# A decoder step on one core: the turn of the keys moved ahead of the feed-forward product, the window mask written by TensorE instead of ScalarE

## The reference, cut to what matters

```python
q = l2norm(q) * qs                     # per head of 64; k in the same way
q = q * cos * scale + rotate_half(q) * sin * scale
sim = einsum('bhwie,bhwje->bhwij', bq, bk2) * QK_SCALE   # windows of 32, keys of own and last window
sim = where(mask, -finfo.max, sim)
attn = softmax(sim, -1)
out = einsum('bhwij,bhwje->bhwie', attn, bv2)
x = attn_layer(shift_tokens(x), ...) + x
x = ffn_layer(shift_tokens(x), ...) + x      # ffn: layernorm * g + b, W1, a * gelu(gate), W2
```

## Time and profile before

| what | us |
|---|---|
| three runs, median | 2246.75 (2243.56 to 2249.29) |
| the profiled execution | 2244.96 |
| its span, first to last instruction | 2243.2 |
| busy: PE / DVE / ACT / POOL | 2034.3 / 1359.3 / 1328.8 / 1079.3 |

### The profile page before, as it was taken

The page is one execution under the profiler, slowest core; times in us unless marked ns, Lnnn a source line. Parts: engine busy times, 40 slices in busy tenths (PEclk is TensorE's granted clock), DMA queues, the critical chain, the costliest instruction groups (busy, mean ns, idle before and its releaser), DMA issues.

```text
span 2243.2 us, 73622 instructions
## 1 busy us (share of the span) xinstructions
PE 2034.3 (91%) x32680; PEld 1198.6 (53%) x32680; DVE 1359.3 (61%) x1663; ACT 1328.8 (59%) x1640; POOL 1079.3 (48%) x708
## 2 busy tenths in 40 slices
PE   8999998779999999999999999999999999999987
PEld 4655655345555555555555555555555555555553
DVE  1444444566666666666766666666676666666662
ACT  4444354365666666656666666666666666666664
POOL 0000000377555555655656555655565656555550
PEclk9999999799999999999999999999999999999999
DMA  3000000022223222232322222222222223222220
GB/s 104 2 1 1 2 19 29 19 58 67 59 60 94 68 68 58 59 87 58 77 59 59 77 68 74 62 58 67 78 75 66 62 59 96 68 67 59 59 58 20
DMA packets 81912, 128.04 MB, mean 57 GB/s; under 512 B 17214, under 2 KB 28092, under 8 KB 81468
## 3 DMA queue, kind: packets, MB, share of 16 engines
q1 hardware_dynamic: 81596, 123.33, 21.2%
HBM read 21.55 MB, written 1.05 MB: 10 GB/s over the span
## 4 chain that ended last, share of the span: by engine, by line
PE 66%; ACT 14%; issue 8%; DVE 7%; POOL 3%; SPq 0%; POOLq 0%; DMA 0%; ACTq 0%; DVEq 0%
PE ps L598 14%; PE ps L624 8%; PE ps L602 7%; PE ps L662 5%; PE ps L679 5%; PE ps L655 5%; ACT KT L962 4%; PE ps L414 4%; PE ps L642 3%; PE ps L607 2%; PE ps L611 2%; DVE work L1055 2%; POOL work L1377 2%; DVE work L1052 2%; ACT ps L953 2%
## 5 line engine op out<-in xcount | busy, mean ns | idle before, releaser
L1377 POOL TENSOR_TENSOR work<-work,RS 128x1024 f32<-128x1024 f32 x192 | 361.6, 1904 | 313.3 <-ACT RS L996 313.3
L602 PEld LDWEIGHTS ps<-ident,work 128*128 128x128 f32 x3072 | 343.6, 142 | 149.3 <-issue 71.0
L1052 DVE TENSOR_TENSOR work<-ps,work 128x1024 f32<-128x1024 f32 x192 | 230.8, 1202 | 311.4 <-ACT work L975 300.0
L602 PE MATMUL ps<-ident,work 128*128 128x128 f32 x3072 | 392.7, 276 | 27.0 <-ACT work L949 12.2
L1371 POOL TENSOR_TENSOR work<-work 128x1024 f32<-128x1024 f32 x96 | 226.2, 2356 | 370.0 <-DVE work L1055 370.0
L598 PE MATMUL ps<-WK,XS 128*128 128x512 f32 x384 | 189.5, 616 | 51.0 <-ACT KT L962 51.0
L1055 DVE TENSOR_TENSOR work<-ps,work 128x1024 f32<-128x1024 f32 x192 | 233.1, 1214 | 0.0
L1091 DVE TENSOR_REDUCE SS<-work 128x16 f32<-128x1024 f32 x192 | 232.1, 1209 | 0.0
L1364 POOL TENSOR_TENSOR work<-work 128x1024 f32<-128x1024 f32 x96 | 226.1, 2355 | 5.7 <-DVE work L1055 5.7
L662 PEld LDWEIGHTS ps<-work 64*32 64x32 f32 x12288 | 136.0, 106 | 163.2 <-issue 106.2
L922 ACT ACTIVATE work<-ps 128x1024 f32<-128x1024 f32 x96 | 98.1, 1022 | 208.7 <-PE ps L662 206.9
(11 more groups left out here) (184 smaller groups left out, 3102.2 us busy)
## 6 DMA issues: line engine op xcount, KB each, us to landing
work<-work SPq DMA_DIRECT2D x576, 128.0 KB
work<-work SPq DMA_DIRECT2D x336, 64.0 KB
WQ<-in_wqkv SPq DMA_DIRECT2D x6, 512.0 KB, 3.6
WK<-in_wqkv SPq DMA_DIRECT2D x6, 512.0 KB, 4.2
WV<-in_wqkv SPq DMA_DIRECT2D x6, 512.0 KB, 3.6
WO<-in_wo SPq DMA_DIRECT2D x6, 512.0 KB, 3.8
work<-ZR SPq DMA_DIRECT2D x48, 64.0 KB
W<-in_w SPq DMA_DIRECT2D x6, 341.0 KB, 3.0
```

What stands on the lines that cost most here:

```text
L602: m = nc.tensor.transpose(flat(R)[:, t * 128:t * 128 + 128], src[:, t * 128:t * 128 + 128], ident[:, :])
L1052: V.tensor_tensor(h16(cos_part[:, j, :]), h16(flat(src)), rotary_tabs[:, at:at + 64].unsqueeze(1).broadcast_to([PARTS, 16, 64]), ALU.mult) ...
L1377: U.tensor_tensor(h16(qk_norm[:, j, :]), h16(cos_part[:, j, :]), inv_norms[:, j, :].unsqueeze(2).broadcast_to([PARTS, 16, 64]), ALU.mult). ...
```

## The change

It changes the order of instructions and moves two pieces of work to another engine:

- PE: the turn of the heads goes ahead of the V projection. The turn of the keys goes ahead of the feed-forward piece, right behind the V projection. The turn of the queries and the K projection stay behind the feed-forward piece.
- The mask: ACT's copy L953 goes. PE puts the mask into bank_x with two bf16 matmuls of 128 x 512 (identity times a broadcast mask) behind the K projection and ahead of the scores; for this the mask is copied to bf16 once by DVE, and PE waits on `values_copied`.
- ACT: the copy of the turned heads (L949) goes ahead of the copy of the values (L942). The load of the gelu table at n = 1 goes behind the copy of the turned keys. `ffn_affine` goes; DVE's `norm` multiplies by g at once and adds b in a second instruction.
- Feed-forward at n = 1: PE makes `hid(1)` whole behind the scores, then the gate of chunk 2 between the weighing's halves and its value at the end. DVE's `gated(1)` goes behind the scores' shift.

```diff
 # PE, step
+                if d:
+                    pe.wait_ge(heads_copied, g - 2)
+                    turn(bank_y, heads).then_inc(heads_turned, 1)
                 if b:
                     pe.wait_ge(wv_loaded, 16 * ((g - 1) // 16 + 1))
...
                     m.then_inc(values_ready, 1)
-                if d:
-                    pe.wait_ge(heads_copied, g - 2)
-                    turn(bank_y, heads).then_inc(heads_turned, 1)
+                if b:
+                    pe.wait_ge(k_normed, g)
+                    if d:
+                        pe.wait_ge(heads_turned_copied, g - 2)
+                    turn(bank_y, qk_norm[:, 1, :]).then_inc(k_turned, 1)
                 if f is not None and n == 0:
                     centre(f)
...
                 if b:
-                    pe.wait_ge(k_normed, g)
-                    if d:
-                        pe.wait_ge(heads_turned_copied, g - 2)
-                    turn(bank_y, qk_norm[:, 1, :]).then_inc(k_turned, 1)
                     if a:
                         pe.wait_ge(q_sin, g + 1)
                     pe.wait_ge(q_normed, g)
...
                     pe.wait_ge(k_turned_copied, g)
                     pe.wait_ge(q_turned_copied, g)
-                    pe.wait_ge(mask_seeded, g)
+                    pe.wait_ge(mask_ready, 1)
+                    pe.wait_ge(values_copied, g)
+                    for q in range(2):
+                        mm(bank_x[:, q, :].rearrange('p (c k) -> p c k', k=64), ident_bf16[:, :], window_bf16[:, 0 if nb == 0 else 1, :].unsqueeze(1).broadcast_to([PARTS, 8, 64]), start=True, stop=False, skip_group_check=True)
...
                     pe.wait_ge(hidden_gated, 3 * f + 1)
-                    hid_gate(1, bank_f)
+                    hid(1, bank_f)
...
-                    hid_value(1, bank_f)
+                    pe.wait_ge(gate_gelu, 3 * f + 2)
+                    hid_gate(2, bank_f)
...
                     pe.wait_ge(hidden_gated, 3 * f + 2)
-                    hid(2, bank_f)
+                    hid_value(2, bank_f)
 # ACT, step
-                if f is not None and n == 1:
-                    ffn_affine(f)
...
-                if b:
-                    act.wait_ge(values_ready, g)
-                    if due(g - 1):
-                        act.wait_ge(windows_loaded, 160 * (g - 1))
-                    A(v_rows[:, (n - 1) % 2, :], flat(bank_x), ACT.Copy).then_inc(values_copied, 1)
                 if d:
                     act.wait_ge(heads_turned, g - 2)
...
                 if b:
-                    act.wait_ge(values_copied, g)
-                    seed = window_mask[:, 0 if n == 1 else 1, :]
-                    A(bank_x.rearrange('p q (c k) -> p (q c) k', k=64), seed.unsqueeze(1).broadcast_to([PARTS, 16, 64]), ACT.Copy).then_inc(mask_seeded, 1)
+                    act.wait_ge(values_ready, g)
+                    if due(g - 1):
+                        act.wait_ge(windows_loaded, 160 * (g - 1))
+                    A(v_rows[:, (n - 1) % 2, :], flat(bank_x), ACT.Copy).then_inc(values_copied, 1)
                 if f is not None and n == 0:
                     square(f)
-                if f is not None and n == 1:
-                    nc.scalar.preload_act_table_set(GELU)
                 if b:
                     act.wait_ge(k_turned, g)
...
+                if f is not None and n == 1:
+                    nc.scalar.preload_act_table_set(GELU)
 # DVE
             def norm(f):
                 dve.wait_ge(ffn_inverse, f + 1)
                 if due(f):
-                    dve.wait_ge(ffn_input, f)
-                V.tensor_tensor(normed[:, :], bank_f[:, 1, :], spread[:, :], ALU.mult).then_inc(ffn_normed, 1)
+                    dve.wait_ge(hidden_ready, 3 * f)
+                V.scalar_tensor_tensor(out=normed[:, :], in0=bank_f[:, 1, :], scalar=layer_vecs[:, f // 4 * 9 + 6:f // 4 * 9 + 7], in1=spread[:, :], op0=ALU.mult, op1=ALU.mult).then_inc(ffn_normed, 1)
+                dve.wait_ge(ffn_normed, f + 1)
+                V.tensor_scalar(ffn_in[:, :], normed[:, :], layer_vecs[:, f // 4 * 9 + 7:f // 4 * 9 + 8], None, ALU.add).then_inc(ffn_input, 1)
...
-                if f is not None and n == 1:
-                    gated(f, 1, bank_f)
                 if b:
                     dve.wait_ge(scores_ready, g)
...
+                if f is not None and n == 1:
+                    gated(f, 1, bank_f)
                 if a:
                     sums(1, k_squared, k_sums, g)
```

More of the change, by code:

```diff
@@ L146, in decoder @@
     ident_bf16 = nc.alloc_sbuf_tensor('ident_bf16', [PARTS, 128], BF16)
+    window_bf16 = nc.alloc_sbuf_tensor('wmb', [PARTS, 2, 64], BF16)
     causal_bf16_mask = nc.alloc_sbuf_tensor('mkb', [PARTS, 128], BF16)
@@ L293, in decoder @@
     windows_loaded = nc.alloc_semaphore('windows_loaded')
-    mask_seeded = nc.alloc_semaphore('mask_seeded')
+    mask_ready = nc.alloc_semaphore('mask_ready')
     q_sums = nc.alloc_semaphore('q_sums')
@@ L910, in inverse @@
                 A(spread[:, :], spread[:, :], ACT.Exp, scale=-0.5).then_inc(ffn_inverse, 1)
[L912 to L916, removed]
             def copy_heads(g):
@@ L1322, in _ @@
             dve.wait_ge(constants_loaded, 16 * 9)
+            V.tensor_copy(window_bf16[:, :, :], window_mask[:, :, :]).then_inc(mask_ready, 1)
             cross()
```

## The result

The changed kernel takes 2351.23 us (median; 2335.81 to 2354.75), against 2246.49 for the kernel before timed beside it: a ratio of 1.0455, with a 95% interval of 1.0417 to 1.0494. It is slower, as forecast, and 21 us above the predicted 2330. The profiled execution took 2347.74 us with a span of 2345.3 (before: 2244.96 and 2243.2).

What follows compares the result with a forecast made beforehand. PE's program order bounds the kernel. Steps n = 0 to 3 change by + 0.90, - 0.46, + 2.34, + 1.11, + 3.89 per pass, + 85.6 over 22; early steps + 1, "issue" - 3: 2330 us, range 2298 to 2368.

Steps and rivals of the forecast that it cites:

- The main step: Keys' turn ahead of the feed-forward piece: PE stands still 1.0, 1.4, 2.1, 1.0 us for POOL's keys at n = 0 to 3.
- The mask: Two bf16 matmuls on PE ahead of the scores: 0.52 us added at n = 1, 2 and 3, hidden at n = 0.
- The regrouping at n = 1: Feed-forward behind the K projection at n = 1: gating wait of 0.70 us per pass ends, about 0.1 new gelu wait.
- The 3 us taken off for "issue": PE's waits that no engine explains, some 21 us: 3 us taken off the sum as falling into the waits for POOL.
- The heads' turn ahead of the values: Heads' turn ahead of the V projection on PE, with ACT's copies swapped: free, as the heads' copy is done before the keys.
- DVE's added instruction: DVE's addition per pass, 0.54 us, at the end of n = 0: costs nothing; 13 us without its cover.
- The ends: The parts before and behind the steps: they don't change by 1 us.
- 1 us earlier: Rival: POOL's pair comes 1 us earlier in every step, so it evens out at 2243 us; chance 0.03.
- The clock's rival: Rival: the wait at n = 2 also lowers PE's clock in every pass, 1.65 us each, 36 in all, 2366; chance 0.14.
- The sign set for the clock's rival: If the waits for POOL are there and the full passes' granted clock is below 0.98, the clock's rival is the case.
- The rival that DVE slows POOL: Rival: DVE's addition slows POOL's product at n = 1 by 0.54 us, 12 us over the passes, 2342; chance 0.04.
- The first rival: Rival: ACT, relieved of the mask copy, gives inverse norms earlier; PE never waits for POOL, 39 us faster, 2205; chance 0.08.

Runs made afterwards that it cites:

- the fastest version: Changed kernel with the keys' turn back behind the feed-forward piece, mask ahead of the K projection, gelu's table load behind ACT's copy of queries at n = 1: 2198.15 us.

## Why the prediction held, and where its sizes were off

**The main step held to about a tenth of a microsecond.** The turn waits for POOL in every step, because POOL's pair starts where it did. The forecast put the K projection at t0 + 9.07, 9.37, 10.95 and 9.82; the undisturbed steps have 9.05, 9.50, 10.96 and 9.79. At n = 1 it is 0.13 later because POOL's pair takes 3.88 us there and not 3.77 (see the small terms). The wait of the projection for ACT's copy stayed at n = 0 alone, 0.82 us, behind the square. The waits for POOL add up to 108 us, not 120: a wait counts only from the end of the last product's tail, 0.17 us after the point from which the prediction counted. That changes no start.

"Undisturbed" in the table means a step without an "issue" pause and without a drop of the clock, behind a step that has none either.

| step | before | forecast | after, undisturbed |
|---|---|---|---|
| n = 0 | 16.26 | 17.16 | 17.14 |
| n = 1 | 20.55 | 20.09 | 19.84 |
| n = 2 | 18.16 | 20.50 | 20.36 |
| n = 3 | 17.40 | 18.51 | 18.32 |
| pass | 72.37 | 76.26 | 75.66 |

**The mask was priced too high.** The pair does hold the scores back by 0.53 us (1774.52 to 1775.05), as the row said. But directly behind the projection it starts 1.72 us after the projection's start, while the scores before came 1.89 after it (1776.80 to 1778.69): the product's tail of 0.17 now lies under the mask. That is 0.36 net at n = 2, and so at n = 1 and n = 3, where 0.52 was put in; over the passes 0.16 x 3 x 22 = 10.6 us too much. The scores before, at n = 1 and 2:

```profile
1758.75 0.86 PE L655 MATMUL ps<-KT,work 64*32 64x64 f32 x64
...
1778.69 0.86 PE L655 MATMUL ps<-KT,work 64*32 64x64 f32 x64
```

The estimate of 0.43 by the Trainium skill's issue gap ("TensorE: Matmul & The Clock Gate", Back-to-back issue gap) lies between the two, the 0.53 and the 0.36.

**The regrouping at n = 1 gave a little more.** From the K projection to the end of the step it takes 10.34 us undisturbed (19.84 - 9.50), where 10.72 was forecast. Of the difference 0.16 is the mask again (2.24 us from the projection to the scores, 1750.81 to 1753.05, against 1.88 before, 1756.87 to 1758.75), 0.1 is the new wait on the gelu, which doesn't show at all, and 0.08 is that the wait taken away was 0.78 in the pass used, not 0.70. That leaves 0.04.

**The clock was the largest mis-sized term.** The undisturbed passes explain 3.29 x 22 = 72.4 of the 92.8 us, where 85.6 were forecast; drops of the clock explain 22.1 - 3.4 = 18.7; some 2 I can't assign. The prediction had the price right (1.65 against 1.70 per drop), but treated the drop as a separate case, all or none, and left it out of the sum, since the clock had stayed up behind 1.85 us in an early step. It came in 13 passes of 22. So part of the near hit is luck, two errors against each other: 13 us too much for the steps (10.6 of them the mask), 19 too little for the clock.

**Small terms.** The 3 us taken off for "issue" were wrong: 21.5 us before, 21.1 after. The heads' turn ahead of the values was costed at nothing, and rightly, given the swap on ACT; the run with the turn alone has neither, and there PE waits 92.5 us for the heads' copy. DVE's added instruction does slow POOL, but little. In 6 of the 22 passes the addition (0.49 us) runs on into the first product of POOL's pair at n = 1, by 0.22 to 0.27 us, and that product takes 1.98 to 2.03 us; where they overlap by 0.05 or less, it takes 1.90, as it always did before. In the pass shown:

```profile
1743.12 0.49 DVE L1075 TENSOR_SCALAR YN<-YR,vec 128x512 f32<-128x512 f32 x1
```

That is 0.12 us where the rival put 0.54, and some 0.7 us over all passes where it put 12, so that the mean of POOL's products barely moves (1908 ns, 1905 before). The Trainium skill ("GPSIMD Engine Reference", Key points) has POOL contend with certain of DVE's instructions; the trace agrees, with 2.03 us against 1.90.

The ends were forecast unchanged and grew by 9.3 us: 3.4 in the attention stage ahead, which the change doesn't touch, 2.1 in the first eight steps (1 forecast), 3.8 in the last steps. Last, were called 22 full passes; the stretch holds 87 steps, one short of that. No term was worked out from its length.

**The rivals.** That the keys come in time, or 1 us earlier, is refuted by POOL's rows. The clock's rival is the case in 13 of 22 passes. The forecast and it together are what happened. The sign set for the clock's rival, a granted clock below 0.98 in the full passes, did not come (0.99): 22 drops of 1.7 us each would bring the mean just under 0.98, 13 do not. The rival that DVE slows POOL is the case too, at about a twentieth of its price. The first rival's K projection at t0 + 8.05 at n = 0 is not the sum given for it, which makes 7.06 (4.41 + 0.86 + 0.87 + 0.87 + 0.05); 8.05 comes out only if ACT's square still holds PE. With the pair starting where it did, nothing hangs on that.

## What to carry to other kernels

An instruction that is moved forward in an in-order queue takes its wait with it, and the wait then holds everything behind it: look up when its operand comes, counted from the step's start, before moving it. Work that stands in front of such a wait is its cover, and a small job without a partner (here a mask of 0.5 us) is best put into a wait that is there anyway; with the turn left where it was, that place for the mask took the kernel from 2241 to 2212 us (1.3%). Where PE is left idle for about 2 us per pass, check the granted clock behind the wait, and count its price into the sum.

## What the runs showed of the hardware

The granted clock fell to 0.50 for 3.4 us behind PE's waits of 2.11 us at n = 2 in 13 of 22 passes. It did not fall behind 1.85 us in an early step, nor behind the 1.40 at n = 1, nor behind 1.5 in the kernel with POOL's order turned; in the run with the turn alone it also fell behind 1.92, but stayed up behind 2.11 in 12 of 22 passes. It also fell behind shorter pauses: 1.66 and 1.71 us in the scores of n = 1, with the mask ahead of the K projection, and in the kernel before behind 0.90 and 0.56 us within one weighing (the drop at 1228.9 us). So the length of the last wait alone does not decide.

```profile
1226.65 0.41 PE L662 MATMUL ps<-work 64*32 64x64 f32 x19 [0.90 <-DVE work L1055]
1227.62 0.69 PE L662 MATMUL ps<-work 64*32 64x64 f32 x45 [0.56 <-issue]
```

In the changed kernel, passes with and without a drop have the same work and the same wait, and come in groups (three without, three with, two without, five with, three without, five with, one without). The four executions of the changed kernel lie 19 us apart (2335.81 to 2354.75), with mean clocks of 0.980 in the shortest and 0.971 to 0.974 in the others. What decides whether a pass is hit stays open.

Nine extra matmuls of 0.23 us each (2.11 for nine) made the full passes 25 us shorter, by keeping PE busy through the wait.

PE's pauses that no engine explains, 0.2 to 1.7 us, mostly in the scores and the weighing, took 21 us in the kernels before and after, 37 with the turn put back (7 of them in front of the mask), 23 in the fastest version. Part of them at n = 1 went with the later table load; what the rest are stays open.
